# Differential attention in a four-part transformer kernel: additions, products and normalisation move from VectorE to GpSimd and ScalarE

## What is computed

```python
xn = (x - mean) * rsqrt(var + eps) * bn_gamma + bn_beta      # over all tokens
q1, q2, k1, k2 = (heads(xn @ w.T) for w in (q1_w, q2_w, k1_w, k2_w))   # 16 heads of 16
v = heads(xn @ v_w.T)                                          # 16 heads of 32
att1 = softmax(q1 k1' / 4);  att2 = softmax(q2 k2' / 4)
lam = exp(sum(lq1*lk1)) - exp(sum(lq2*lk2)) + LAMBDA_INIT
y = (att1 - lam * att2) @ v
y = y * rsqrt(mean(y*y) + eps) * subln_w * (1 - LAMBDA_INIT)
return y @ c_w.T                                               # added to x
```

## Time and profile before

| what | value |
|---|---|
| median of 3 runs | 4386.19 us (4371.55 to 4391.42) |
| the profiled execution, its own time | 4380.7 us |
| its span in the trace | 4379.0 us |
| busy: TensorE / VectorE / ScalarE / GpSimd | 85% / 56% / 37% / 7% |
| the attention's scores (L1131), first and last start | 666.6 and 1513.8 us |

### The profile page before, as it was taken

One profiled execution on the slowest core, in us unless ns is written; L12 is line 12 of the kernel. 1 busy time (PEld: TensorE's weight loads), 2 busy tenths in 40 slices (PEclk: granted clock), 3 DMA queues, 4 the chain that ended last, 5 costly groups with the idle time before them and its releaser, 6 DMA issues. The chain is left out here.

```text
span 4379.0 us, 111137 instructions
## 1 busy us (share of the span) xinstructions
PE 3742.5 (85%) x45369; PEld 2335.2 (53%) x45369; DVE 2454.6 (56%) x8606; ACT 1617.5 (37%) x4197; POOL 320.5 (7%) x122
## 2 busy tenths in 40 slices
PE   7895758888888767999999948989999989999899
PEld 3223422222222234656666524446888888888666
DVE  6224546777777515444444474444777767777554
ACT  3474523444444304555454422213222222222222
POOL 0000002333333300000000000000000000000000
PEclk8697879999999868999999979997555555555799
DMA  1000010000000020010001000001000000000000
GB/s 59 1 2 9 1 49 1 1 1 1 1 1 1 1 88 20 24 35 20 20 20 37 3 22 0 0 0 50 4 4 4 4 5 4 4 5 4 5 7 9
DMA packets 33775, 57.74 MB, mean 13 GB/s; under 512 B 5302, under 2 KB 27787, under 8 KB 32396
## 3 DMA queue, kind: packets, MB, share of 16 engines
q1 hardware_dynamic: 32882, 49.35, 3.2%
q10 hardware_dynamic: 418, 1.58, 0.1%
HBM read 48.77 MB, written 2.16 MB: 12 GB/s over the span
## 5 line engine op out<-in xcount | busy, mean ns | idle before, releaser
L1284 DVE TENSOR_REDUCE diff_mx<-diff_m_ps 128x1 f32<-128x512 f32 x512 | 329.9, 686 | 261.8 <-PE diff_m_ps L1137 259.9
L1131 PE MATMUL diff_s_ps<-diff_qk 32*128 32x512 f32 x1024 | 308.3, 675 | 127.0 <-DVE diff_mx L1284 122.7
L1675 PE MATMUL moe_y_ps<-moe_wparts,moe_hparts 128*128 128x256 f16 x3456 | 395.7, 273 | 16.8 <-DVE moe_hparts L1809 16.8
L1662 PE MATMUL moe_h_ps<-moe_xparts,moe_wparts 128*128 128x512 f16 x1728 | 386.7, 384 | 24.8 <-issue 14.4
L2401 PE MATMUL gru_sums<-gru_take,gru_u 128*128 128x4 f16 x12288 | 399.4, 166 | 3.8 <-issue 3.3
L2401 PE MATMUL gru_sums<-gru_keep,gru_u 128*128 128x4 f16 x12288 | 399.5, 166 | 2.3 <-DVE gru_keep L2471 2.2
L1233 ACT ACTIVATE diff_probs<-diff_s_ps 128x512 f32<-128x512 f32 x512 | 277.9, 595 | 319.9 <-PE diff_s_ps L1131 319.6
L1675 PEld LDWEIGHTS moe_y_ps<-moe_wparts,moe_hparts 128*128 128x128 f16 x3456 | 332.3, 98 | 81.9 <-DVE moe_hparts L1809 36.8
L2401 PEld LDWEIGHTS gru_sums<-gru_keep,gru_u 128*128 128x128 f16 x12288 | 370.5, 104 | 3.6 <-issue 2.7
L2401 PEld LDWEIGHTS gru_sums<-gru_take,gru_u 128*128 128x128 f16 x12288 | 367.6, 104 | 3.9 <-issue 3.4
L1722 ACT ACTIVATE moe_hf<-moe_h_ps,moe_b,moe_hscale 128x512 f32<-128x512 f32 x288 | 224.1, 778 | 365.7 <-PE moe_h_ps L1662 365.7
(11 more groups left out here) (408 smaller groups left out, 5588.9 us busy)
## 6 DMA issues: line engine op xcount, KB each, us to landing
moe_raw<-in_L_ffn_W SPq DMA_DIRECT2D x18, 1024.0 KB, 6.8
lora_w<-in_L_cond_w_R SPq DMA_DIRECT2D x1, 4096.0 KB
stream_b<-in_x SPq DMA_DIRECT2D x4, 512.0 KB, 10.4
hyp_wf<-in_L_cond_w_f SPq DMA_DIRECT2D x2, 1024.0 KB, 8.4
stream_b<-in_xT SPq DMA_DIRECT2D x1, 2048.0 KB, 13.1
moe_raw<-in_L_ffn_sW SPq DMA_DIRECT2D x2, 1024.0 KB, 6.2
tree_win<-in_L_ffn_W_in_T SPq DMA_DIRECT2D x1, 2048.0 KB, 7.6
tree_wout<-in_L_ffn_W_out_T SPq DMA_DIRECT2D x1, 2048.0 KB, 15.7
```

The lines of the kernel that those rows point to most:

```text
L1131: pe.matmul(s_ps[:, (n + hh) % 3, :], k[at:at + 32, kt * P:(kt + 1) * P], q[at:at + 32, :], start=True, stop=True, tile_position=(at, 0)). ...
L1284: dve.tensor_reduce(mx[:, i % 2, kt, at:at + 1], m_ps[:, m % 3, :], X_AXIS, ALU.max).then_inc(ph.maxes_ready, 1)
L1662: last = pe.matmul(h_ps[:, m % RING, :], w1p(k, pw)[:, c, m * P:(m + 1) * P], xparts[:, px, c, g * T:(g + 1) * T], start=(j == 0 and c == ...
L1675: last = pe.matmul(y_ps[:, g % 2, t, :], hparts[:, g % 2, px, m, t * P:(t + 1) * P], w2p(k, pw)[:, m, :], start=(j == 0 and m == 0), stop= ...
```

## The change

- The multiplication by minus lambda (L1309) is gone from VectorE. ScalarE's copy of `o_ps` becomes an activation with a scale for each partition, `weigh`: 1 for the first 64 rows, minus lambda for the others. `weigh` is filled once, by two small copies ahead of the pipeline.
- The addition (L1317) and the square (L1318) go to GpSimd, between its additions of probabilities. VectorE sums the squares at s = 2 and no longer at s = 0.
- GpSimd adds all four key tiles in a chain of three 128x2048 additions into `sums`, which has two buffers (used by item in turn); the sums then take four products and not eight.
- Per batch, ScalarE normalises x, and GpSimd multiplies y by its factors, one quarter in each of four items. The v tiles move to items 2, 3, 4 and 6 of a batch (s = 7), the transpositions of y to items 2 to 5 of the next batch (s = 3), the output products to its items 5 (s = 7) and 6 (s = 3). The loops run three items further at the end.

```diff
@@ TensorE
-                            pe.wait_ge(ph.added, 2 * i)
+                            pe.wait_ge(ph.added, (TT - 1) * i)
                             pe.wait_ge(*free)
-                            for half in range(2):
-                                for j in range(4):
-                                    last = pe.matmul(mix[32 * j:32 * j + 32, :], ones[:, 0:32], halves[:, half, j, :],
-                                                     start=(half == 0), stop=(half == 1), tile_position=(0, 32 * j))
+                            for j in range(4):
+                                last = pe.matmul(mix[32 * j:32 * j + 32, :], ones[:, 0:32], sums[:, (i - 1) % 2, j, :],
+                                                 start=True, stop=True, tile_position=(0, 32 * j))
@@ ScalarE
-                                act.wait_ge(ph.added, 2 * (i - 1) + kt // 2 + 1)
+                                act.wait_ge(ph.added, (TT - 1) * (i - 1) + max(kt, 1))
...
-                            act.copy(oT[:, (i - 1) % 2, :], o_ps[:, :]).then_inc(ph.o_taken, 1)
-                        if s == 1 and done_batch is not None and rel == 1:
+                            act.activation(oT[:, (i - 1) % 2, :], o_ps[:, :], ACT.Identity, scale=weigh[:, 0:1]).then_inc(ph.o_taken, 1)
+                        if s == 3 and i >= 0 and rel == 1 and i // PAIRS + 1 < B:
+                            normalize(i // PAIRS + 1)
+                        if s == 3 and done_batch is not None and rel == 1:
                             act.wait_ge(ph.squares_ready, PAIRS * (done_batch + 1))
@@ VectorE
-                        if s == 0 and 0 <= i - 2 < ITEMS:
+                        if s == 2 and 0 <= i - 2 < ITEMS:
                             db, dh = divmod(i - 2, PAIRS)
+                            dve.wait_ge(ph.squared, i - 1)
                             dve.tensor_reduce(ms[:, db % 2, 0, :, 2 * dh:2 * dh + 2], sq[:, :, :, :], X_AXIS, ALU.add
...
-                            dve.wait_ge(ph.sums_read, i)
-                            step(dve.tensor_scalar(r[:, :, 2:4], r[:, :, 2:4], neg_lam, None, ALU.mult))
                         if s == 6 and 0 <= i - 1 < ITEMS:
                             dve.wait_ge(ph.o_turned, i)
+                            dve.wait_ge(ph.sums_read, i)
+                            if i >= 2:
+                                dve.wait_ge(ph.combined, i - 1)
...
-                        if s == 7 and 0 <= i - 1 < ITEMS:
-                            dve.wait_ge(ph.o_read, i)
-                            two = y[:, b % 2, :, 2 * h:2 * h + 2, :]
-                            step(dve.tensor_tensor(two, part[:, :, 0:2, :], part[:, :, 2:4, :], ALU.add))
-                            step(dve.tensor_tensor(sq[:, :, :, :], two, two, ALU.mult))
@@ GpSimd
+                def gather(i, kt):
+                    total = sums[:, i % 2, :, :]
+                    if kt == 1:
+                        pool.wait_ge(ph.probs_ready, 2 * STEPS * i + 2 * TT)
+                        if i >= 2:
+                            pool.wait_ge(ph.summed, i - 1)
+                        pool.tensor_tensor(total, probs[:, 0, :, :], probs[:, 1, :, :], ALU.add).then_inc(ph.added, 1)
+                    else:
+                        pool.wait_ge(ph.probs_ready, 2 * STEPS * i + TT * (kt + 1))
+                        pool.wait_ge(ph.added, (TT - 1) * i + kt - 1)
+                        pool.tensor_tensor(total, total, probs[:, kt, :, :], ALU.add).then_inc(ph.added, 1)
+
+                for i in range(ITEMS + 5):
+                    if i < ITEMS:
+                        gather(i, 1)
+                        gather(i, 2)
+                    if 0 <= i - 1 < ITEMS:
+                        b, h = divmod(i - 1, PAIRS)
+                        two = y[:, b % 2, :, 2 * h:2 * h + 2, :]
+                        pool.wait_ge(ph.o_read, i)
+                        pool.tensor_tensor(two, part[:, :, 0:2, :], part[:, :, 2:4, :], ALU.add).then_inc(ph.combined, 1)
+                        pool.wait_ge(ph.combined, i)
+                        if i >= 2:
+                            pool.wait_ge(ph.squares_ready, i - 1)
+                        pool.tensor_tensor(sq[:, :, :, :], two, two, ALU.mult).then_inc(ph.squared, 1)
+                    done_batch, rel = finished(i)
+                    if done_batch is not None and 1 <= rel <= 4:
...
+                        pool.tensor_tensor(heads, heads, ms[:, done_batch % 2, 0, :, 4 * k:4 * k + 4].unsqueeze(3).to_broadcast(
+                            [P, TT, 4, VD]), ALU.mult).then_inc(ph.y_ready, 1)
+                    if i < ITEMS:
+                        gather(i, 3)
```

More of the change, by code:

```diff
@@ L1003, in differential_block @@
         one = ph.sb("one", [P, 1])
+        weigh = ph.sb("weigh", [P, 1])
         eps = ph.sb("eps", [P, 1])
@@ L1051, in _ @@
                     dve.tensor_copy(one[32 * j:32 * j + 32, :], ident[0:32, MAX_ROW:MAX_ROW + 1])
+                dve.tensor_copy(weigh[0:64, :], ones[0:64, 0:1])
+                dve.tensor_copy(weigh[64:P, :], lamc[64:P, 0:1])
                 step(dve.tensor_scalar(sub[:, :], sub[:, :], 1.0 - LAMBDA_INIT, None, ALU.mult))
@@ L1062, in differential_block, with diff_stream @@
         nc.all_engine_barrier()
-        diff_stream(nc, ph, ident, ones, one, eps, affine, lamc[:, 0:1], wqk, wv, wc, mx, xcT, x1T)
+        diff_stream(nc, ph, ident, ones, one, eps, affine, weigh, wqk, wv, wc, mx, xcT, x1T)
         ph.rejoin()
-def diff_stream(nc, ph, ident, ones, one, eps, affine, neg_lam, wqk, wv, wc, mx, xcT, x1T):
+def diff_stream(nc, ph, ident, ones, one, eps, affine, weigh, wqk, wv, wc, mx, xcT, x1T):
     with ExitStack() as inner:
@@ L1077, in diff_stream @@
         probs = sb("probs", [P, TT, 4, T])
-        halves = sb("halves", [P, 2, 4, T])
+        sums = sb("sums", [P, 2, 4, T])
         oT = sb("oT", [P, 2, T])
@@ L1110, in _ @@
                 free = None
-                for i in range(-AHEAD, ITEMS + 4):
+                for i in range(-AHEAD, ITEMS + 7):
                     done_batch, rel = finished(i)
@@ L1199, in _ @@
                             free = (ph.o_read, i)
-                        if done_batch is not None and rel in (1, 2) and s in (3, 7):
-                            k = 2 * (rel - 1) + s // 7
+                        if done_batch is not None and 2 <= rel <= 5 and s == 3:
+                            k = rel - 2
                             pe.wait_ge(ph.y_ready, 4 * done_batch + k + 1)
@@ L1209, in _ @@
                             free = (ph.y_taken, 4 * done_batch + k + 1)
-                        if done_batch is not None and rel == 3 and s in (3, 7):
-                            c = s // 7
+                        if done_batch is not None and (rel, s) in ((5, 7), (6, 3)):
+                            c = rel - 5
                             pe.wait_ge(*free)
@@ L1221, in _, with normalize @@
             def _(act):
-                for i in range(-AHEAD, ITEMS + 4):
+                def normalize(b):
+                    for c in range(DC):
+                        last = act.activation(xn[:, b % 2, c, :], xcT[:, c, b * T:(b + 1) * T], ACT.Identity,
+                                              bias=affine[:, 1, c:c + 1], scale=affine[:, 0, c:c + 1])
+                    last.then_inc(ph.xn_ready, 1)
+                normalize(0)
+                for i in range(-AHEAD, ITEMS + 7):
                     done_batch, rel = finished(i)
@@ L1264, in _ @@
             def _(dve):
-                step = Steps(dve, ph.stream_step)
-                def normalize(b):
-                    for c in range(DC):
-                        last = dve.tensor_scalar(xn[:, b % 2, c, :], xcT[:, c, b * T:(b + 1) * T], affine[:, 0, c:c + 1],
-                                                 affine[:, 1, c:c + 1], ALU.mult, ALU.add)
-                    last.then_inc(ph.xn_ready, 1)
-                normalize(0)
-                for i in range(-AHEAD, ITEMS + 4):
+                for i in range(-AHEAD, ITEMS + 7):
                     done_batch, rel = finished(i)
-                    b, h = divmod(i - 1, PAIRS)
                     for s in range(STEPS):
@@ L1293, in _ @@
                             dve.tensor_tensor(q, q, mix[:, :], ALU.subtract).then_inc(ph.max_taken, 1)
[L1294 to L1296 removed]
+                        if s == 4 and done_batch is not None and rel == 1:
                             dve.wait_ge(ph.rooted, done_batch + 1)
[L1298 to L1303 removed]
+                            dve.reciprocal(ms[:, done_batch % 2, 0, :, :], ms[:, done_batch % 2, 1, :, :]
+                                           ).then_inc(ph.factors_ready, 1)
                         if s == 5 and 0 <= i - 1 < ITEMS:
@@ L1328, in _ @@
             def _(pool):
-                for i in range(ITEMS):
-                    for half in range(2):
-                        pool.wait_ge(ph.probs_ready, 2 * STEPS * i + 2 * TT * (half + 1))
-                        if i >= 1:
```

(5 more changed lines are left out.)

30 lines of the change are left out of this document (13 added, 17 removed).

## The result

The changed kernel takes **4254.03 us** (median of 4 runs, 4245.21 to 4271.07) against 4378.87 us for the kernel before on the same chip (median of 4, 4365.18 to 4391.42). The ratio is 0.972, with a 95% interval of 0.9675 to 0.9765: faster by 125 us, where 124 were forecast (4386.19 to 4262).

What follows compares the result with a forecast made beforehand. TensorE's order with its short loop to VectorE, which pauses under GpSimd's additions, sets the pace. Items 2 to 28 give -119 us and the ends -5: -124, 4257 us profiled, plus 5.5 for the median: 4262 us, range 4240 to 4312.

Steps and rivals of the forecast that it cites:

- Step 0: First score step of an item: loses VectorE's pause behind L1317, from 6.37 to 3.98 us, -2.39 us.
- Step 6: Score step s = 6: loses the pause behind L1309, from 3.60 to 2.64 us, -0.96 us.
- Step 4: Score step s = 4: four sum products where it had eight, -0.92 us, leaving 2.86 us.
- Batch work: Items 2 to 28: v tiles 12 us, output products 11, ScalarE's normalisation and table loads 6; 29 us added in all.
- Clock: TensorE in items 2 to 28: 2.4 GHz expected nearly throughout, 14 us of slower clock left out; if kept, 14 us later.
- The window: Items 2 to 28 of the attention: 616 us for 735, so -119 us.
- ends: Start and end of the attention's pipeline, outside items 2 to 28: together -5 us.
- What was costed at nothing: GpSimd's small operations (0.6 us each), VectorE's wait for squares, ScalarE's scaled copy, L1312 under an addition: covered by slack, 0.
- Rival 1: VectorE's SBUF reads, L1312 included, wait under GpSimd additions: 1.6 us in some 30 items, 48 us, 4310 us; chance 0.13.
- Rival 2: GpSimd's small operations each take 4.5 us, an item 22.6 us: some +40 us, 4300 us; chance 0.05.
- Rival 3: GpSimd becomes the bound; with small operations at 7.5 us, 42 us slower than before, 4428 us; chance 0.02.
- Rival 4: TensorE waits elsewhere: pauses go but another wait holds the steps, time within 22 us of before; chance 0.02.

Runs made afterwards that it cites:

- experiment 2: Kernel before, with addition L1317 and square L1318 on VectorE directly behind L1312, in GpSimd's gap, one step earlier: 4317.67 us, 0.9834.
- experiment 3: Changed kernel with the addition and the square back on VectorE at s = 7, gone from GpSimd: 4312.61 us, 0.9846 of the kernel before.
- experiment 6: Changed kernel with the addition and the square on VectorE at s = 2 of the next item, in GpSimd's gap: 4260.24 us, 0.9717 of the kernel before.
- experiment 1: Kernel before, with only the multiplication by minus lambda (L1309) moved into ScalarE's copy: 4363.1 us, 0.9934.
- experiment 4: Changed kernel with its four sum products issued twice: 4285.27 us, 0.9759 of the kernel before.
- experiment 5: Kernel before, with minus lambda in ScalarE's copy and addition and square moved into GpSimd's gap on VectorE, nothing moved to GpSimd: 4283.88 us, 0.9789.
- experiment 10: Changed kernel measured once more, unchanged, on another chip: 4263.84 us (6 runs), 0.9721 of the kernel before.

## Why the prediction was right

- **Step 0, -2.39 us:** 3.98 us, as forecast. Experiments 2, 3 and 6 show the cause: an addition (4.67 us for 0.42) or a square (4.62 for 0.42) of SBUF inputs on VectorE stands still while GpSimd adds, and moving it in time does what moving it to GpSimd does.
- **Step 6, -0.96 us:** 2.65 against 2.64 forecast. Experiment 1 alone gives it.
- **Step 4, -0.92 us:** -0.85, to 2.93 us; experiment 4 gives 0.86. The halved time of the sums was 0.06 us too generous. Step 7 is 2.08 and not 2.05. That makes an item 21.86 instead of 21.73, and 27 of them 3.5 us more than forecast.
- **Batch work, 29 us:** 28. A v tile step is 2.98, +0.90, 12 of them 10.8 us (12 forecast). An output product's step is 4.70, +2.62, four of them 10.5 (11). The rest, 618.2 - 27 x 21.86 - 21.3 = 6.7 us, is ScalarE's table loads and normalisation (6 forecast), nearly all in items 9, 17 and 25.
- **Clock:** the 14 us left out are gone; the granted clock is 1.00 in the window. Before, it fell to 1.2 GHz thirteen times for 3.4 us in these items. The size of 14 fits experiment 5: it saves 84.3 us there, of which 27 x 2.77 = 74.8 are the steps; the other 9.5 are the clock's, less some 4 us of batch work that had hidden behind the pauses. One step at a lower clock is left, in item 17, behind ScalarE's 5.2 us.
- **The window:** -116.4 for -119. The **ends**: -10.0 for -5 (before the first scores -2.0, items 0 and 1 -2.6, from item 29 on -5.4). Items 0 and 1, which I took to save 1.9, saved 2.6; the fill, for which I had 0.5 more, became 2.0 shorter; the tail gained 5.4 where my terms for it came to 3.5. The fill, from the first load to the first scores, is 76.0 to 76.1 us before and in experiments 1, 2 and 5, and 73.8 to 74.1 in the change and in experiments 3, 4, 6 and 10: it goes with the normalisation of x on ScalarE, which no run took by itself. Relative to its size this was the worst term of the sum. That -126.4 came so close to -124 is partly luck: the two errors, 2.6 short and 5 over, cancel.
- **What was costed at nothing:** the small GpSimd operations are 727 and 613 ns, 1.34 us in an item for the 1.2 of the estimate; y's quarters 1047 ns. GpSimd's slack covered them.
- **Rival 1** (L1312, now L1311, waits under an addition) is refuted: the shortest is 691 and the longest 692 ns in all 32, and 31 of them run wholly under an addition. It reads PSUM and one SBUF tile. The rule of the Trainium skill, SBUF - State Buffer, "Who interferes with whom", which would leave it free, holds here. Its advice in Perfetto Trace Analysis, "Optimizing Scalar/DVE Operations", that moving work between the two might not help, did not come true here: between experiment 3 and the change, addition and square go from VectorE to GpSimd, and the stretch is 70.8 us shorter. But experiment 6 gets the same without the move. **Rivals 2 and 3** needed small operations of 4 and 7 us; they take 0.6 to 1.05. **Rival 4** is refuted by the steps.
- **The absolute number:** I put the profiled execution of after at 4257 and its median 5.5 us above. It was 4271.07, and the median 17 us *below*. That step was not sound: the distance of one execution from the median is not a property of the kernel, but of the stretch ahead, below.

Of the change's 126.4 us, experiment 5, which moved no work to GpSimd, has 98.75: the two pauses and the clock that they cost, less 0.5 us an item for its longer step 7. The remaining 27.6 us are a sum in which the cheaper sums are the largest term but not the only one. In items 2 to 28 the change is 32.1 us ahead of experiment 5: 27 x 0.86 = 23 for the cheaper sums and 27 x 0.51 = 14 for step 7 at 2.08 and not 2.59, less 5 for batch work (28.0 us beyond the plain items, 23.1 in experiment 5); at the ends it loses 4.5 again. The 14 us are no reward for a lighter VectorE as such: experiment 6 has the same two operations on VectorE and a step 7 of 2.08 us. What counts is again where they stand. Two gains that an engineer might have had for two small edits, a scale in a copy and one step number, are nearly four fifths of this large change.

## What to carry to other kernels

A mean that is far above its neighbour of the same shape (4399 against 425 ns here) can be a pause and not a cost: find in the timeline what ends at the same moment, and move the instruction out from under it, before moving it to another engine. Here TensorE's odd steps took 2.08 us whether they held a transposition or nothing beyond the scores, so that there was nothing to gain by emptying them; finer waits moved the wait and brought 0.6 us of 21.9; products moved from the full steps into the held ones brought 2.3. When an in-order engine is held by a loop through another, try that, and count first what else already lives in that slack. Compare the stretch that the change touches, from one untouched marker to the next, when code elsewhere varies from run to run.

## What the runs showed of the hardware

**A clock that differs from run to run in the same code.** The hyperbolic block ahead of the attention is the same in all kernels. From 200 to 300 us TensorE is busy without a gap in each of these windows, of before and of after:

```profile
200.00:300.00 100.00, 100.00 (x715) 28.11 (x712) 21.64 (x37) 80.92 (x84) 0.00 (x0) 0.96 0.00 1
```

```profile
200.00:300.00 100.00, 100.00 (x594) 25.21 (x587) 16.57 (x29) 67.23 (x70) 0.00 (x0) 0.77 0.00 1
```

The granted clock is 0.96 in one and 0.77 in the other, and 715 and 594 products get done. In the twelve profiles of this study the attention began at 580 to 582 us in four (granted clock there 1.00), at 590.5 in one (0.96), and at 604 to 610 in seven (0.76 to 0.79), although the code up to there is the same. That is up to 30 us of span, as much as experiment 1 is worth. The only kernel profiled twice, the change, began at 607.2 and 603.9. That runs of one kernel differ in the same way is likely from their mean clock, which every run has: it is 0.813 to 0.816 in the profiles with the early start and 0.807 to 0.812 in those with the late one, and of the six runs of experiment 10 one has 0.816 and takes 4238.83 us, the others 0.808 to 0.810 and 4259.85 to 4270.24. What makes the chip choose was not found, and no run tried it.

**Small operations on GpSimd are not priced by size alone.** 2048 elements for each partition take 4522 ns, 2.2 ns each. 256 take 613 ns in the square, which reads one tile in runs of 64 and writes a contiguous one, and 727 ns in the addition, whose inputs and output are all in runs of 64; 512 with a broadcast factor take 1047 ns, 2.0 ns each.

**Eight numbers for each partition are enough to pause.** L1309 multiplies an SBUF tile of 128x8 by a column. The one time that it met no GpSimd addition it took 0.23 us; the other 31 times it lasted until 0.03 us behind the addition's end, in experiment 2 too (that addition ends at 1081.89):

```profile
1079.84 2.08 DVE L1309 TENSOR_SCALAR diff_r<-diff_r,diff_lamc 128x8 f32<-128x8 f32 x1
```

Not all that VectorE reads from SBUF waits. In the same kernel 26 sums of squares (L1288, one SBUF input, 128x256) start under a GpSimd addition and take 407 to 411 ns, as long as the others, and none of the 512 maxima, which read PSUM, takes longer than 693 ns. In the changed kernel the same holds for the 31 L1311 and for 6 subtractions (L1297, 677 to 679 ns), each with one input in PSUM and one in SBUF.
